# A table more looked up whole in the first unit of a DLRM tower, and its late splits one place forward

## What is computed

```
e = stack([tbl_k[ids[:, k]] for k in range(26)], axis=1)      # 2048 x 26 x 128
T = concatenate([r_dense[:, None, :], e], axis=1)             # 27 rows per sample
Z = einsum('bnd,bmd->bnm', T, T);  z = Z[:, upper triangle]   # 351 products
h = relu(concatenate([z, r_dense], 1) @ W_top1 + b_top1)      # 512
h = relu(h @ W_top2 + b_top2)                                 # 256
y = h @ W_top3
```

## Time and profile before

| | before |
|---|---|
| median of 3 runs | 367.7 us (367.35 to 368.36) |
| the profiled execution | 367.51 us, span 365.7 us |
| busy share PE / DVE / ACT / POOL | 94% / 61% / 47% / 70% |
| first cycle (products of unit 0 to products of unit 1) | 43.41 to 80.06 |
| a steady cycle | 40.6 us |

### The profile page before, as it was taken

The page is one execution under the profiler, slowest core; times in us unless marked ns, Lnnn a source line. Parts: engine busy times, 40 slices in busy tenths (PEclk is TensorE's granted clock), DMA queues, the critical chain, the costliest instruction groups (busy, mean ns, idle before and its releaser), DMA issues.

```text
span 365.7 us, 9897 instructions
## 1 busy us (share of the span) xinstructions
PE 343.7 (94%) x4042; PEld 321.2 (88%) x4042; DVE 223.3 (61%) x786; ACT 172.5 (47%) x220; POOL 255.7 (70%) x263
## 2 busy tenths in 40 slices
PE   3997898879899999999999999999999999999976
PEld 1887798869889999999989998999999998998866
DVE  3989969976826485556927394656828493622311
ACT  4266737553456244553466153643476154435111
POOL 6788877777777777777777777777777777775000
PEclk9999999989999999999999999999999999999986
DMA  7996232353525522354225522462225321544030
GB/s 206 262 257 189 66 124 62 92 144 109 179 59 135 170 58 52 87 130 147 58 52 138 167 60 50 103 182 79 60 52 136 96 60 52 120 112 86 21 61 1
DMA packets 45878, 39.07 MB, mean 107 GB/s; under 512 B 32930, under 2 KB 39113, under 8 KB 45834
## 3 DMA queue, kind: packets, MB, share of 16 engines
q1 hardware_dynamic: 36014, 21.40, 22.1%
q0 software_dynamic: 8192, 16.79, 17.4%
q10 hardware_dynamic: 1628, 0.25, 0.5%
HBM read 32.40 MB, written 6.02 MB: 105 GB/s over the span
## 4 chain that ended last, share of the span: by engine, by line
PE 82%; DMA 6%; ACT 6%; DVE 3%; issue 2%; ACTq 0%; SPq 0%; DVEq 0%
PE look_ps L747 35%; PE gram_ps L773 15%; PE mlp_ps L793 13%; PE look_ps L757 7%; PE mlp_ps L803 7%; DMA ids_near<-ids_rows 2%; ACT T L614 2%; PE look_ps L738 2%; DVE hot L464 2%; DMA ids_rows<-rows 1%; DMA dots_last<-gram 1%; ACT T L606 1%; ACT tab_hi L582 1%; PE mlp_ps L814 1%; DMA ids_all<-in_ids_dram 1%
## 5 line engine op out<-in xcount | busy, mean ns | idle before, releaser
L418 POOL DMA_INDIRECT rows<-in_tbl_dram,ids_all x240 | 236.9, 987 | 73.2 <-issue 71.3
L464 DVE TENSOR_SCALAR hot<-ids_near 125x256 fp32r<-125x256 f16 x640 | 149.1, 304 | 41.9 <-PE look_ps L747 35.4
L747 PE MATMUL look_ps<-hot,tab_hi 125*128 125x256 f32 x616 | 154.4, 290 | 6.4 <-DVE tab_lo L447 2.2
L747 PE MATMUL look_ps<-hot,tab_lo 125*128 125x256 f32 x616 | 150.2, 283 | 0.0
L747 PEld LDWEIGHTS look_ps<-hot,tab_hi 125*128 125x128 f32 x616 | 117.8, 191 | 8.2 <-issue 3.8
L747 PEld LDWEIGHTS look_ps<-hot,tab_lo 125*128 125x128 f32 x616 | 118.1, 192 | 0.1
L614 ACT COPY T<-look_ps 128x384 f32<-128x384 f32 (+1 forms) x80 | 85.3, 1109 | 69.1 <-PE look_ps L757 69.0
L488 DVE COPY gram<-gram_ps 128x432 f32<-128x432 f32 x64 | 38.8, 607 | 68.6 <-PE gram_ps L773 66.5
L606 ACT COPY T<-look_ps 128x512 f32<-128x512 f32 x32 | 38.7, 1208 | 74.2 <-PE look_ps L747 69.0
L773 PEld LDWEIGHTS gram_ps<-T 128*54 128x54 f32 x2048 | 54.5, 131 | 8.2 <-issue 4.5
L773 PE MATMUL gram_ps<-T 128*54 128x54 f32 x2048 | 57.8, 215 | 1.9 <-DVE gram L488 1.2
(11 more groups left out here) (72 smaller groups left out, 137.3 us busy)
## 6 DMA issues: line engine op xcount, KB each, us to landing
dots<-gram SPq DMA_DIRECT2D x28, 182.2 KB
ids_near<-ids_rows SPq DMA_DIRECT2D x7, 640.0 KB, 6.2
rows<-in_tbl_dram,ids_all POOLq DMA_INDIRECT x240, 2.6
T<-in_tbl_dram SPq DMA_DIRECT2D x5, 448.0 KB
pairs<-dots SPq DMA_DIRECT2D x14, 117.0 KB
rows<-in_r_dense_dram SPq DMA_DIRECT2D x16, 64.0 KB
gram<-in_tbl_dram SPq DMA_DIRECT2D x2, 448.0 KB
pairs<-dots SPq DMA_DIRECT2D x7, 104.0 KB
```

Source lines behind the costliest of these rows:

```text
L418: pool.indirect_dma_start(rows[:, t % 2, place[n], :], None, tables[n - 1], bass.IndirectOffsetOnAxis(ap=index[:, n - 1:n].bitcast(U32), a ...
L464: eq = nc.vector.tensor_scalar(hot[:VP, at % 2, c], ids_near[:VP, u % 2, k], float(c), None, ALU.is_equal)
L747: mm = pe.matmul(dst, w[:VP, k, c], hot[:VP, slot, c], start=(c == 0 and half == 0), stop=(c == CH - 1 and half == 1))
```

## The change

Table 7 joins tables 1, 3 and 5 in `WHOLE`. Its raw rows lie in `w2`. In the first unit it is looked up whole, ahead of table 6 (`LOOKS_FIRST`), and in the later units the looks are (8, 9), (1, 3), (5,), (7,) instead of (7, 8), (9, 1), (3,), (5,). DVE and ACT get four late splits in the first cycle in place of three, and the splits of tables 1, 3 and 5 stand one place of the looks earlier than they did. SP waits for the split of table 7 before it loads W2.

```
-    LOOKS_FIRST = ((1, 0), (3, 2), (5, 4), (6, 7), (8,), (9,))
-    LOOKS = ((0, 2), (4, 6), (7, 8), (9, 1), (3,), (5,))
-    WHOLE = (1, 3, 5)
+    LOOKS_FIRST = ((1, 0), (3, 2), (5, 4), (7, 6), (8,), (9,))
+    LOOKS = ((0, 2), (4, 6), (8, 9), (1, 3), (5,), (7,))
+    WHOLE = (1, 3, 5, 7)
...
-                     table_at(h1[:].rearrange("p f q -> p (f q)"), 0)]
+                     table_at(h1[:].rearrange("p f q -> p (f q)"), 0), table_at(w2[:].rearrange("p c f -> p (c f)"), 0)]
...
                     load_pair_weights(1)
+                    sp.wait_ge(lo_ready, split_count(WHOLE[3]))
                     sp.dma_start(w2[:], W2.rearrange("(c p) f -> p c f", p=P)).then_inc(weights_landed, 16)
...
             compare(0, 5)
-            for at in range(6, K):
-                if at > 6:
-                    split(looked_first[at])
-                compare(0, at)
+            compare(0, 6)
+            split(8)
+            compare(0, 7)
+            split(9)
+            compare(0, 8)
+            compare(0, 9)
             compare(1, 0)
...
-                for at in range(2, 6):
+                for at in range(2, 5):
                     compare(u + 1, at)
-                if u > 1:
-                    y_out(u - 2)
-                dense_out(u, 1)
                 if u == 0:
                     lead(WHOLE[0])
-                compare(u + 1, 6)
-                if u == 0:
+                    compare(u + 1, 5)
                     rest(WHOLE[0])
-                if u > 0:
+                    dense_out(u, 1)
+                    lead(WHOLE[1])
+                    compare(u + 1, 6)
+                    rest(WHOLE[1])
+                    gram_out(u, 1)
+                    lead(WHOLE[2])
                     compare(u + 1, 7)
-                gram_out(u, 1)
-                if u == 0:
-                    lead(WHOLE[1])
+                    rest(WHOLE[2])
+                    lead(WHOLE[3])
+                    compare(u + 1, 8)
+                    rest(WHOLE[3])
...
             look_out(0, 2)
             turn_out(0, 0, 1)
-            hi_out(7)
             make_relative(1)
             hi_out(8)
+            hi_out(9)
             look_out(0, 3)
             turn_out(0, 0, 2)
-            hi_out(9)
             look_out(0, 4)
```

More of the change, by code:

```diff
@@ L522, in _ @@
             compare(0, 0)
-            split(looked_first[1])
+            split(0)
             compare(0, 1)
-            split(looked_first[3])
+            split(2)
             compare(0, 2)
             compare(0, 3)
-            split(looked_first[5])
+            split(4)
             compare(0, 4)
-            split(looked_first[6])
+            split(6)
             compare(0, 5)
-            for at in range(6, K):
-                if at > 6:
-                    split(looked_first[at])
-                compare(0, at)
+            compare(0, 6)
[4 more added lines that the diff above has]
+            compare(0, 9)
             compare(1, 0)
@@ L540, in _ @@
                 gram_out(u, 0)
-                for at in range(2, 6):
+                for at in range(2, 5):
                     compare(u + 1, at)
-                if u > 1:
-                    y_out(u - 2)
-                dense_out(u, 1)
                 if u == 0:
                     lead(WHOLE[0])
-                compare(u + 1, 6)
-                if u == 0:
+                    compare(u + 1, 5)
                     rest(WHOLE[0])
-                if u > 0:
-                    compare(u + 1, 7)
-                gram_out(u, 1)
-                if u == 0:
-                    lead(WHOLE[1])
+                    dense_out(u, 1)
[4 more added lines that the diff above has]
+                    lead(WHOLE[2])
+                    compare(u + 1, 7)
+                    rest(WHOLE[2])
+                    lead(WHOLE[3])
+                    compare(u + 1, 8)
+                    rest(WHOLE[3])
+                else:
+                    compare(u + 1, 5)
+                    if u > 1:
+                        y_out(u - 2)
+                    dense_out(u, 1)
+                    compare(u + 1, 6)
                     compare(u + 1, 7)
[L557 to L560, removed]
+                    gram_out(u, 1)
+                    compare(u + 1, 8)
                 compare(u + 1, 9)
-                if u == 0:
-                    rest(WHOLE[2])
                 if u + 2 < UNITS:
@@ L686, in _ @@
                 look_out(u + 1, 1)
+                if u == 0:
+                    hi_out(WHOLE[0])
                 turn_out(u, 1, 3)
@@ L689, in _ @@
                 if u == 0:
-                    hi_out(WHOLE[0])
+                    hi_out(WHOLE[1])
                 look_out(u + 1, 2)
@@ L699, in _ @@
                 if u == 0:
-                    hi_out(WHOLE[1])
+                    hi_out(WHOLE[2])
                 look_out(u + 1, 3)
@@ L704, in _ @@
                 if u == 0:
-                    hi_out(WHOLE[2])
+                    hi_out(WHOLE[3])
                 look_out(u + 1, 4)
```

## The result

| | before | changed |
|---|---|---|
| median of 22 runs each | 366.28 us (363.69 to 369.67) | 368.67 us (365.53 to 373.62) |
| changed / before | | 1.005 (95%: 1.0027 to 1.0074) |
| the profiled execution | 367.51 us, span 365.7 | 370.13 us, span 368.3 |

The kernel became slower by 0.5%, 1.8 us (1.0 to 2.7). The forecast was +1.74, with 367.8 to 371.1 us as its range. The ratio leaves out runs that took over 1.5% longer than the fastest of their kernel, six of the changed one (their mean granted clock was 0.981 to 0.986) and one of before; with all of them the medians lie 2.4 us apart.

What follows compares the result with a forecast made beforehand. PE, busy throughout every steady cycle, was taken as the bound, with POOL's gathers almost abreast. 0.2 gained in unit 0, 1.49 + 1.69 lost in the first cycle, 1.24 returned: +1.74, 369.4 us, range 367.8 to 371.1.

Steps and rivals of the forecast that it cites:

- the hot row behind the rest: First cycle: DVE builds place 9's hot row after table 7's rest, delaying unit 1's last look by 1.69 us more.
- First unit: Unit 0: DVE loses table 7's split, ACT becomes the late engine; gain 0.2 us, bounds 0 and 0.43.
- The load itself is of the same size, and one place of raw slots becomes another; nothing: Unit 0, loading raw table 7: same load size in another raw slot, so no cost.
- that look stays at 37.2: Unit 0: PE's look of table 8 still waits for ACT's high half, so its start does not move.
- Rival C: Unit 0: raw table 9, now wanted at 33.03, lands late; +4.7 us, 372.4 us; chance 0.04.
- Second gram copy: First cycle: one more split ahead of this DVE copy, less an old 0.78 us wait, delays it; 1.49 us lost.
- The table before last: Unit 1's look before the last waits for DVE until 74.4, hidden under the longer chain ending at 76.58.
- SP: nothing: SP's new wait for table 7's split before W2 costs nothing; SP gets there about 86, the split ends near 77.7.
- The gather gives 1.24 back: Second cycle: PE's 1.24 us wait at 94.57 for tile 3's last gather absorbs that much of the delay.
- The clock: First cycle: the low-clock stretch from 78.0 to 81.5, costing 1.6 us, stays because PE's waits get longer.
- rival A: First cycle: the clock stays high, ending it 1.6 us sooner; +0.14, 367.8 us, no difference; chance 0.14.
- rival D: A second or longer low-clock stretch costs another 1.6 us, 371.0 us; chance 0.12.

Runs made afterwards that it cites:

- e1: The changed kernel with the hot row at place 9 of unit 1 built ahead of table 7's rest: 366.8 us, ratio 0.998 to the kernel before.
- e4: The changed kernel with the small weight loads (some 0.5 MB) issued behind the second dense tile: 366.36 us, ratio 0.999 to the kernel before.
- e5: The kernel before with the small weight loads issued behind the second dense tile: 367.04 us, ratio 1.0016 to the unedited kernel before.

## Why the prediction was right, and where not

The sum, +1.74, met the measured +1.8 (1.0 to 2.7), but two of its terms were off in opposite directions. By the landmarks the terms come to 1.2 or 1.6 lost in the first unit, 2.48 in the first cycle and 1.24 returned, +2.4 to +2.8. The medians of all runs, 2.4 us apart, fit that better. So that the sum lies within 0.1 us of the measured +1.8 is luck; the direction and the hot row behind the rest are not.

*First unit: forecast a gain of 0.2, measured a loss of 1.2 to 1.6* (28.92 to 30.16 and 30.47 behind the first look of table 0). The step that failed is "The load itself is of the same size, and one place of raw slots becomes another; nothing", and with it "that look stays at 37.2", which has table 8's look wait for ACT only. Taking the split of table 7 off DVE moved the wish for raw 8 and raw 9 forward by 3.6 us, and the loads did not move with it. In e1 they landed at 30.97 and 35.45, 9.9 and 8.4 us after SP had issued them; DVE had come to raw 8 at 29.64. In e4, where both are nearly in time, the first unit is 28.75, just what the forecast's gain of 0.2 asks for. Rival C had the mechanism for raw 9, put the whole at +4.7 and gave it 0.04; it came smaller, and for raw 8, which was not considered, as well. Its argument, that the ids issued before raw 9 on the same queue "land at 33.6", shows only that raw 9 comes after that. The rows of before could not have shown when raw 8 lands, since DVE asked for it only at 33.03: here the bound of the nearest row should have been kept as a cost.

In the profiled execution the first look of table 0 itself stood at 16.03, not 14.49. PE began the look before it 0.67 us later, waiting for table 1's raw rows, and then 6.29 us passed until the next look began, instead of 5.42:

```profile
9.74 6.63 PE L746 MATMUL look_ps<-hot,w 125*128 125x256 f32 x16 [2.02 <-DMA w<-in_tbl_dram]
```

Nothing ahead of this look differs between the two kernels, and in e1 and e4 the first look of table 0 is at 14.64 and 14.33, so the 1.5 us are not the change's. Why the look took longer no run shows (in the other executions 4.9 to 5.7 us).

*Second gram copy: forecast +1.49 behind the start of the products, measured +1.00* (63.46 - 43.41 = 20.05 to 67.55 - 46.50 = 21.05). The mechanism stands, one split more ahead of the copy, its price reduced by DVE's old wait of 0.78 us. The three hot rows at places 4, 5 and 6 took 5.12 us in all, where in the kernel before they took 5.70; that makes up the 0.5.

*Hot row behind the rest: forecast 1.69, measured 1.67* by e1 against the changed kernel. From the gram copy to the last look it is 33.25 - 20.05 = 13.20 before and 35.73 - 21.05 = 14.68 after, only 1.48 more: in e1, without this term, the stretch is 12.94. Both terms together: 3.18 forecast, 2.48 measured. The table before last waited too (1.44 us at 77.35, for a hot row that ended at 77.24) and was hidden, as said.

*SP: nothing, right.* W2 goes out at 87.65 (before 88.83).

*The gather gives 1.24 back: right in the main.* No turn of the changed kernel waits in the second cycle; in the kernel before one waits 1.24, in e5 2.49. That the amount is fixed, because the gather "doesn't depend on PE", was too simple: the gather's start hardly moves, but its landing does by about a microsecond (e5). And the second cycle of the changed kernel begins slower than the forecast had it: PE waits 0.42 us for a copy of products at 88.63, and from the start of the products of unit 1 to the next turn it takes 4.39 us, where e4 takes 3.75 and e1 3.52. Why that copy came late the trace doesn't show.

*The clock: wrong for this execution.* The forecast kept the slow stretch after longer waits of PE and named a missing one as a sign of being wrong; the changed kernel's windows row has none:

```profile
78.00:86.00 8.00, 5.13 (x68) 4.71 (x68) 6.46 (x25) 3.87 (x6) 6.17 (x7) 1.00 0.46 123
```

By the forecast's own rival A the changed kernel should then be only 0.14 us slower. It wasn't, and that rests on the errors above: the first unit lost 1.2 to 1.6 us, and from the last look to the turn, the 1.24 left out, the changed kernel is 0.4 us faster than before (16.27 against 16.67) and not 1.6, a part of it taken by the slower products of unit 1. In eight of the 22 runs the mean clock was as low as 0.981 to 0.986, and these took 371.5 us in the mean: rival D, a second slow stretch, put at 371.0 with a chance of 0.12, fits them, though none of them was profiled. The profiled pair adds up so: +3.09 at the products of unit 0, +2.48 to the last look, -0.45 to the products of unit 1 (before's low clock), -1.19 from there to the turn that waited at 94.57 (the fourth transpose of the row at 98.17, at 98.50), +0.14 to the last turn, and -1.47 after it, where the kernel before was granted 0.76 from 350 us on and the changed one 0.91: +2.6.

The chain of the changed kernel in order of time, from the store of the ids to the high halves of tables 8 and 9 (start, duration, what):

```profile
22.08 8.05 DMA ids_rows<-rows
30.15 4.51 DMA ids_near<-ids_rows
34.74 2.43 ACT ids_near L598
37.17 1.89 ACT tab_hi L589 x2
```

The forecast had the high halves end near 37.9; they end at 39.06, 1.2 later, for a first look of table 0 that is 1.5 us later. So ACT's shift was not what held the first unit up; DVE's hot rows were, that of table 6 behind the split of the late raw 8 (PE's look at 36.44), and that of table 8, ready at 40.8, behind the split of the late raw 9 (PE's look at 40.93).

## What to carry to other kernels

When work is taken off an engine at the start of a kernel, everything it asks for later is asked for earlier: look at when each later load really lands, and if the trace can't show it because nobody waited, give it a price. Where a written order puts a step that waits for another engine ahead of a step that waits for nothing, try the swap: that swap was worth 1.7 us of the path here. And before pricing a gain on the engine that is busy all the time, look for a stream beside it that never waits: here the last of 256 gathers lands about half a microsecond before PE wants it (334.39 + 2.6 against 337.47), and of a first cycle shorter by 5 us the profiled execution kept nothing and the runs 2.0 us. Waits for such a stream hide losses too: with one of the two losses left the runs showed none, with both they showed 1.8 us.

## What was not expected of the hardware

- Waits of 1.30 and 2.17 us on PE were followed by the low clock in the kernel before (0.52 granted from 78.0 to 81.5, the 1.2 GHz level); in the changed kernel, waits of 1.65, 1.09, 1.44 and 2.40 us were not. Of the 22 runs of the changed kernel ten had a mean granted clock of 0.995 and took 367.9 us in the mean, six had 0.986 and took 371.1, one had 1.000 and took 365.5. Most of the spread of 8 us goes with the clock; runs of the same 0.995 still lie 4.3 us apart.
- Landings in the first 35 us vary: PE had to wait for table 1's rows until 9.74 in one execution and began at 9.07 in another, though nothing ahead of them had changed, and from the store of the ids to the next step of SP, 5.2 us passed in the kernel before, 8.1 in the changed one and 5.9 in e1, which has the same order of loads.
- Two chips ran the same kernel in 515 and 527 us, with stops of ACT and DVE that nothing in the program released, 20.8 us in the one shown and up to 26.3 us in the others.
